# A float32 megakernel (conditioned mix, one-key attention, grouped convolution, 4-bit linear layer): the exponential of the mixing weights issued earlier, more products that nothing reads before the first z, and a new order of the calls on every engine

## The reference, cut to what matters

```
# stage 1
att   = softmax(MLP(cond))                       # [64, 8], a mixing weight for 8 kernels
m     = einsum('bk,koi,bih->boh', att, weight, x) + (att @ bias_k)
q,k,v = m @ Wq, m @ Wk, m @ Wv (+ biases)         # 32 heads for q, one for k and v
p     = softmax over e of q[s,d,h] * k[s,e] / sqrt(32)
o     = sum over e of p * v                       # copied to all heads: the reference sums q over heads
x     = x + o (each value on 32 neighbours)
# stage 2
u     = conv1d(x, 9 taps, 4 groups) + cond @ c_weight + bias
x     = x + u @ (scale * (int4 weights - zero)) + bias
```

## Time and profile before

| | us |
|---|---|
| median of 3 runs (lowest to highest) | 408.34 (408.29 to 411.07) |
| the execution that was profiled | 410.41 |
| its span, first to last instruction | 408.6 |
| PE busy / DVE busy / POOL busy / ACT busy | 390.6 / 352.2 / 294.1 / 217.6 |
| mean granted clock of TensorE, as a share of the full one | 0.987 |

### The profile page before, as it was taken

How to read it: one execution, slowest core, us unless ns; L and a number is a source line. 1 busy time by engine, 2 the same in 40 slices (tenths; PEclk the granted TensorE clock), 3 DMA queues, 4 the chain that set the end, 5 groups by cost and what they waited for, 6 DMA issues and landing times.

```text
span 408.6 us, 7642 instructions
## 1 busy us (share of the span) xinstructions
PE 390.6 (96%) x2747; PEld 306.1 (75%) x2747; DVE 352.2 (86%) x594; ACT 217.6 (53%) x472; POOL 294.1 (72%) x222
## 2 busy tenths in 40 slices
PE   5985987999999999999999999999999999999997
PEld 4875875878678778787867686878787786878686
DVE  1889998999999999999999899999999998963432
ACT  4535664765746483555656564747092826472600
POOL 6032988988829997589769987679948598519930
PEclk9999888999999999999999999999999999999999
DMA  8994994565176263729855434857146535525112
GB/s 317 408 408 178 346 335 148 171 265 187 45 269 226 93 208 106 262 90 319 288 166 209 127 110 136 310 170 275 55 143 226 168 147 158 184 82 205 56 53 104
DMA packets 24957, 79.20 MB, mean 194 GB/s; under 512 B 6088, under 2 KB 6728, under 8 KB 22984
## 3 DMA queue, kind: packets, MB, share of 16 engines
q1 hardware_dynamic: 24760, 78.32, 54.8%
q10 hardware_dynamic: 144, 0.13, 0.1%
HBM read 61.14 MB, written 17.30 MB: 192 GB/s over the span
## 4 chain that ended last, share of the span: by engine, by line
PE 44%; POOL 5%; issue 3%; DMA 2%; DVE 0%; SPq 0%; POOLq 0%; DVEq 0%
PE p_f L1913 32%; PE p_conv L1888 5%; PE p_conv L1897 4%; PE p_sm L1855 2%; POOL c_lo L594 2%; POOL xc L588 2%; DMA o_dram<-o_sb 1%; POOL xn L603 1%; DMA o_c<-o_dram 1%; POOL xn L610 1%; PE p_conv L1913 0%; PE p_sm L1875 0%; SPq L358 0%; DVE xn L1366 0%; DVE rden L1338 0%
## 5 line engine op out<-in xcount | busy, mean ns | idle before, releaser
L1913 PE MATMUL p_f<-w_ffn,u_hi 128*128 128x512 f32 (+1 forms) x512 | 195.6, 393 | 0.0
L1913 PE MATMUL p_f<-w_ffn,u_lo 128*128 128x512 f32 (+1 forms) x512 | 195.2, 390 | 0.0
L916 ACT ACTIVATE u_sb<-p_conv,u_bias,cols_sb 128x128 f32<-128x128 f32 x256 | 95.1, 481 | 83.3 <-PE p_conv L1897 81.6
L1913 PEld LDWEIGHTS p_f<-w_ffn,u_hi 128*128 128x128 f32 x512 | 96.1, 188 | 29.1 <-issue 9.0
L1913 PEld LDWEIGHTS p_f<-w_ffn,u_lo 128*128 128x128 f32 x512 | 96.1, 188 | 20.4 <-issue 0.8
L594 POOL TENSOR_TENSOR c_lo<-xc,c_hi 128x512 fp32r<-128x512 f32 (+1 forms) x68 | 76.1, 1139 | 23.0 <-ACT c_hi L906 23.0
L603 POOL TENSOR_TENSOR xn<-xn,bias_n 128x1024 f32<-128x1024 f32 x32 | 76.4, 2399 | 19.3 <-DMA xn<-xn_in_in 19.3
L588 POOL TENSOR_TENSOR xc<-xc,o_c 128x512 f32<-128x512 f32 (+1 forms) x68 | 69.6, 1050 | 26.6 <-DMA o_c<-o_dram 22.7
L1366 DVE TENSOR_TENSOR xn<-p_f,xn 128x512 f32<-128x512 f32 x64 | 43.2, 676 | 25.3 <-PE p_f L1913 18.4
L610 POOL TENSOR_TENSOR xn<-xn,o_sb 128x1024 f32<-128x1024 f32 x32 | 61.1, 1920 | 0.8
L895 ACT ACTIVATE prob<-prob 128x1024 f32<-128x1024 f32 (+1 forms) x32 | 34.0, 1063 | 37.4 <-DVE prob L1298 32.8
(11 more groups left out here) (124 smaller groups left out, 370.9 us busy)
## 6 DMA issues: line engine op xcount, KB each, us to landing
xn<-xn_in_in SPq DMA_DIRECT2D x16, 1024.0 KB, 5.7
out<-xn SPq DMA_DIRECT2D x31, 512.0 KB, 5.0
xc<-xc_in_in SPq DMA_DIRECT2D x15, 1040.0 KB, 7.1
xt<-xt_in_in SPq DMA_DIRECT2D x11, 1024.0 KB, 8.4
o_c<-o_dram SPq DMA_DIRECT2D x15, 256.0 KB
xn<-xt_in_in SPq DMA_DIRECT2D x3, 1024.0 KB, 16.6
xn<-wq_in SPq DMA_DIRECT2D x5, 512.0 KB, 8.4
xt<-xt_in_in SPq DMA_DIRECT2D x4, 512.0 KB, 10.9
```

Of the source, the lines that this page charges most:

```text
L916: ins = eng.activation(u_sb[:, g % 2, i * P:(i + 1) * P], p_conv[g][:, i * P:(i + 1) * P], ACT.Identity, bias=u_bias[:, g, bat:bat + 1], s ...
L1913: return mm(ffn_ps(k, part), u[:, (k // TU) % 2, r, t * P:(t + 1) * P], w_ffn[:, r, at:end], **flags)
```

## The change

No function is changed; only the lists of calls are. Three places stand out, the rest is a new order of calls on all engines (some 700 lines of the diff).

- ACT: `exp_att` is issued ahead of `copy_vk`, and DVE unpacks all nibbles directly behind the first sum of heads, for which SP loads `packed` as the third transfer and not the thirteenth.
- PE: 23 calls of `keep_busy(1)` in place of 14. They now also stand between the slices of `z_first`.
- All engines: calls in a new order, of which the first part stands here.

```diff
@@ SP @@
             load_wq(0)
+            load_packed()
             load_wq(1)
...
             load_wq(8)
-            load_packed()
             load_tile(0, 1)
             load_tile(1, 0)
-            load_c_first(0)
             load_conv_weights()
             load_tile(1, 1)
             load_x(2)
             load_x(3)
+            load_c_first(0)
             load_x(4)
             load_x(5)
+            load_bias()
             save_o(0, 0)
-            load_bias()
+            load_c_first(1)
             spread_first(0)
+            load_x(6)
+            load_n(0)
+            load_n(1)
             save_o(0, 1)
-            load_n(0)
-            load_x(6)
-            load_c_first(1)
             spread_first(1)
@@ POOL @@
             add_o(1, 0)
             add_o(1, 1)
+            x_o(0)
+            add_o(1, 2)
+            c_low(1, 0)
             x_bias(1)
-            c_low(1, 0)
-            add_o(1, 2)
             add_o(1, 3)
-            x_o(0)
-            x_o(1)
-            x_bias(2)
             c_low(1, 1)
             c_low(1, 2)
+            x_o(1)
             c_low(1, 3)
-            x_bias(3)
             add_o(2, 0)
             add_o(2, 1)
             add_o(2, 2)
+            c_low(2, 0)
+            x_bias(2)
@@ ACT @@
             keep_bias()
+            exp_att()
             copy_vk()
-            exp_att()
             slices()
...
             z_copy(0)
+            convert_weights(0, 0)
             exp(0, 0)
             exp_first()
+            exp(0, 1)
             z_copy(1)
-            exp(0, 1)
-            z_copy(2)
-            convert_weights(0, 0)
-            z_copy(3)
             exp(1, 0)
             bias_of_u()
+            z_copy(2)
+            exp(1, 1)
+            z_copy(3)
+            z_copy(4)
@@ DVE @@
             sum_heads(0)
+            low_nibbles()
+            high_nibbles()
             logits()
             normal()
             sum_heads(1)
             sum_heads(2)
             sum_heads(3)
-            mark_inexact()
...
             sum_heads(8)
-            low_nibbles()
+            mark_inexact()
             bias_of_qkv(0)
...
             sum_v_first()
-            softmax_top(1)
             divide(0, 0)
             sum_exp(0, 1)
+            softmax_top(1)
...
             sum_exp(1, 0)
-            high_nibbles()
             times_v(1, 0)
-            softmax_top(2)
             sum_v(1, 0)
             divide(1, 0)
             sum_exp(1, 1)
+            softmax_top(2)
...
             subtract(2, 1)
-            turn_u(0, 0)
             softmax_top(3)
             sum_exp(2, 0)
+            turn_u(0, 0)
@@ PE @@
             keep_busy(1)
             keep_busy(1)
             keep_busy(1)
+            keep_busy(1)
+            keep_busy(1)
+            keep_busy(1)
+            mlp(0)
             bias_rows()
-            mlp(0)
+            keep_busy(1)
             mlp(1)
+            keep_busy(1)
+            keep_busy(1)
             mlp(2)
             keep_busy(1)
             keep_busy(1)
             keep_busy(1)
             keep_busy(1)
+            keep_busy(1)
             turn_att()
+            keep_busy(1)
+            keep_busy(1)
+            keep_busy(1)
             z_first(0)
-            z_first(1)
             mixing(0)
             mixing(1)
             mixing(2)
             mixing_bias()
-            keep_busy(1)
-            keep_busy(1)
-            read_flag()
             mixing(3)
             keep_busy(1)
-            keep_busy(1)
-            keep_busy(1)
+            z_first(1)
             keep_busy(1)
             z_first(2)
+            keep_busy(1)
             z_first(3)
+            keep_busy(1)
             z_first(4)
+            keep_busy(1)
             z_first(5)
+            keep_busy(1)
             z_first(6)
-            keep_busy(1)
             z_first(7)
...
             project(1, 1)
+            context()
             mix(1)
             project(2, 0)
             project(2, 1)
-            context()
             project(3, 0)
             project(3, 1)
             mix(2)
             project(4, 0)
             project(4, 1)
-            conv(0, 0)
             project(5, 0)
             project(5, 1)
+            project(6, 0)
+            project(6, 1)
+            mix(3)
+            read_flag()
+            conv(0, 0)
             conv(0, 1)
             conv(0, 2)
             conv(0, 3)
-            project(6, 0)
             edges(0)
-            project(6, 1)
-            mix(3)
             project(7, 0)
             project(7, 1)
             project(8, 0)
+            project(8, 1)
             conv(1, 0)
             conv(1, 1)
             conv(1, 2)
             conv(1, 3)
             edges(1)
-            project(8, 1)
             linear(0, 0)
```

753 lines of the change are left out of this document (375 added, 378 removed).

## The result

The changed kernel takes 405.63 us in the median of 20 runs (403.28 to 412.64), the kernel before 408.78 of 20 runs beside it (406.76 to 411.07): a ratio of 0.9927, interval 0.9907 to 0.9947. The gain is 1.2 to 3.2 us where 7.1 were forecast (408.34 less 401.2), and the single runs of the changed kernel lie further apart than those of the one before. The profiled execution took 407.03 us with a span of 405.2.

What follows compares the result with a forecast made beforehand. Bound: the 72.3 us up to the first linear, plus a block where PE works without a gap. Gain 5.4 + 2.7 = 8.1 us gives 402.3 from the profile, 400.2 from the median, middle 401.2; range 398.5 to 406.3.

Steps and rivals of the forecast that it cites:

- rival D: Whole kernel: nothing is gained at the start and the new order only shuffles, within 1%, 408 us; chance 0.08.
- Part 3: PE from T0: project(7) at 55.9, first linear at 65.1, 7.1 us earlier, "in old times" (T0 left at 22.22).
- T0: Start of attention, the bias of q, k, v on DVE: 22.22 before, forecast at 19.5.
- Part 1: The start up to T0: the last head sum at 18.9 plus 0.62 us gives 19.5, gain 2.7 us.
- The head sums: DVE ahead of T0: packed delays Wq by 1.3 us, sums end 18.5 to 19.0 against 18.3, loss taken as 0.5.
- The clock at the start: PE with 23 keep_busy: high clock by about 10 to 14 us, so PE keeps up with the head sums.
- rival A: PE's start: the clock doesn't rise earlier, T0 at 22.7, total gain 4.9, 404.4 us; chance 0.17.
- High nibbles: DVE's unpacking, moved to the start: 0.67 to 1.50 us there, and 1.4 us leaves the chain behind T0.
- Part 2: DVE from T0 to 72 us: high nibbles leave, the 1.69 us wait goes, turn_u(0,0) moves; together 3.5 us ahead.
- PE keeps 5.4 of 7.1: Behind 72 us: PE keeps between 3.5 and 7.1 us of its lead, the middle taken as 5.4.
- Rival B: Behind the first linear: DVE bounds all, PE keeps 3.5 of 7.1, gain 6.2, 403.1 us; chance 0.19.
- C: DVE from 90 to 360 us: reordered calls wait at the queue's head, slower, for example 416 us; chance 0.04.

Runs made afterwards that it cites:

- second comparison: The unedited changed kernel run again against the kernel before, with the experiments: 407.28 us against 408.45, ratio 0.9946.
- a_oldpe: Changed kernel with PE's calls up to z_first(7) as in the kernel before (14 keep_busy, old places; read_flag at its new place): 407.27 us, ratio 0.9948.
- a_save: Changed kernel with load_n(1) issued behind save_o(0,1) on SP: 403.79 us, ratio 0.9883.
- a_fill: Changed kernel with products that nothing reads on PE, 12 ahead of mix(1) and 7 ahead of mix(2): 407.54 us, ratio 0.9942.
- best: Changed kernel with packed behind load_wq(8), both unpackings behind divide(0,0), convert_weights(0,0) behind z_copy(1), load_n(1) behind save_o(0,1): 405.28 us, ratio 0.9928.
- after_look: The changed kernel, unedited, a third profile: 406.03 us, span 404.2.
- after_again: The changed kernel, unedited, run and profiled again: 407.28 us, ratio to the kernel before 0.9946.
- a_x7: Changed kernel with load_x(7) issued ahead of save_o(0,1) on SP: 407.85 us, ratio 0.9968.
- best_fill18: The kernel of best with products that nothing reads on PE, 12 ahead of mix(1) and 18 ahead of mix(2): 403.97 us, ratio 0.9853.

## Why the prediction was wrong

The direction held, and so did the place: what is won is won ahead of the first linear. The size did not: 401.2 forecast, 405.6 measured, inside the range (the second comparison's 407.3 is outside it), and by under 1%, which I had given to rival D. The step that failed is Part 3, project(7) "at 55.9", through the tile that it waits for and the clock that it then runs at; T0, Part 1, fell short beside it.

- **The head sums (part 1, "taken as 0.5").** This term was mis-sized: they end at 20.05, 1.75 us later, and the experiment without the early packed has them at 17.66. I delayed only the last piece; pieces before it came too late for their sums as well, so DVE waited twice, 0.80 and 1.25 us. T0 is 20.81, 20.94 and 20.46 in three profiles, for 19.5: 1.0 to 1.4 us. Why that is more than the 1.3 us of the transfer put ahead of them, no run takes apart.
- **The clock at the start** rose by about 10 us, as forecast, and mixing(3) ended at 13.4 to 14.5. But it was not what T0 waited for: with the old products, where the weight loads of a column sum still take 0.40 us for four at 18.0, T0 is 21.14 (a_oldpe), 0.3 us later than with the new ones. And rival A is part of the truth in another form: the clock may rise too early, be lost at turn_att, and T0 then comes at 24 (a_save, a_fill). I had costed the products both ways ("4.7 us of PE at the low clock and half at the high one") but not asked whether, at half their time, they still cover the wait for turn_att.
- **High nibbles.** 0.69 us, by the lower bound (0.67). In all four profiles in which it starts 1 us behind POOL's `prob` it takes 1.50 and ends 0.5 to 0.6 us behind that one; behind divide(0,0), with no POOL instruction beside it, 0.69 (best). At the start it isn't alone, but there it came first, and it is POOL that took longer. POOL in the first profile of the changed kernel:

```profile
6.98 0.75 POOL L572 CAST rest_hi<-zp 128x128 fp32r<-128x128 f32 x1
7.82 0.75 POOL L574 TENSOR_TENSOR rest_lo<-zp,rest_hi 128x128 fp32r<-128x128 f32 x1
```

  The same two take 0.29 and 0.40 us in the kernel before, where DVE unpacks nothing beside them. The Trainium skill, SBUF — State Buffer, section "SBUF: two separate sides", has an exclusive lock by which the later of the two blocks; the rows agree, in both directions.
- **Part 3, project(7) "at 55.9" in old times**, 53.2 with the forecast T0. This is the step that failed. I had seen save_o(0,1) behind load_n(1) and priced it for conv(1) alone (63.6); that load_x(7) stands behind the same spread was missed. Measured 57.38: 1.3 of the difference from T0, 2.9 from the tile. Then project(7) at the low clock: 4.51 for 2.86, 1.6 us. Together 5.8, all of the difference between 62.4 and 68.17. In the two other profiles of the same kernel the tile costs less: T0, tile and what follows project(7) come to 1.0, 1.8 and 1.6 us in after_look, 1.4, 0.3 and 0.4 in after_again. Without the tile the step was right: in a_x7 project(7) waits for DVE alone and starts 33.8 us behind T0, where the forecast had 33.7. Putting load_n(1) behind save_o(0,1) takes the wait for the tile away (a_save, best, best_fill18); what that is worth at the end isn't shown, as a_save has 0.9883 and best, with the same repair among others, 0.9928.
- **The clock in the middle.** I took it as given (2.9 "or 4.5 where the clock is low"). It differed by execution: the first linear was 64.60, 66.72 or 68.17 with T0 at 20.5 to 20.9. In two profiles of before it varied by 0.1.
- **Part 2.** The 1.69 us wait of turn_u(1,0) for u_copy(1,0) is gone as forecast. But a new one of 2.45 us stands a few rows earlier: it is turn_u(0,3) that waits, for u_copy(0,3), which the new order on ACT has behind z_copy(7), and so behind project(7). So a late project(7) holds up DVE too. DVE in the first profile of the changed kernel:

```profile
63.64 0.46 DVE L1352 STREAM_TRANSPOSE p_conv<-u_sb 128x256 f32<-128x256 f32 x1 [2.45 <-ACT u_sb L916]
...
69.74 0.78 DVE L1352 STREAM_TRANSPOSE p_conv<-u_sb 128x256 f32<-128x256 f32 x2
```

  POOL's wait for xn ahead of c_low(1,1) is gone as forecast; it waits 2.00 us for c_high there now.
- **"PE keeps 5.4 of 7.1"**, a loss of 1.7 us (the middle of 3.5 and 7.1 is 5.3), came out about right in size: the end is 337.3 us behind the first linear on average where it was 335.9, a loss of 1.4. That is luck, as the reason was another: I had DVE lag by more the further PE runs ahead, and the loss doesn't grow with the lead. What it consists of is open; the waits of PE behind 72 us explain 0.5 us of it in the first profile. Rival B, a loss of 3.6, fell (DVE's busy time from 60 to 360 is 285.80, before 286.12), and C, slower, with it; D's size came, but not its mechanism, as T0 and the first linear are both earlier. With a first linear at 62.4 and 337 us behind it the span would have been 399.4; with the mean of the three measured, 66.5, it is 403.5, and 405.3 with the 1.8 us around the span. On top of that come the runs with the late start, 9 of 32, which no term of the sum holds.
- **Profile against median.** Two profiled executions of before took 410.4 and 409.8, its median is 408.8: the middle that I took between them was right in kind. The changed kernel's three took 407.0, 403.4 and 406.0.
- Attention's last o is at 356.63, for a forecast of 351 to 354, 2.8 earlier than before.

What stays open: why the clock rises before 5.2 us in some executions and near 10 in others; where the spread of the kernel before comes from, whose runs have a mean granted clock of 0.983 to 0.992 and take 406.2 to 412.3 us; and what of the 0.75% between best and best_fill18 is the full clock and what the small number of runs on another chip. That falls follow idle time of PE is borne out by best_fill18, where the waits are filled and all six runs are without a fall; which idle time brings one is not (a_fill fell after two waits of 0.5 us, best held through 1.74). That the late start costs some 3 us is seen in T0 of a_save and a_fill (24.0 and 24.4) and in the medians of the 9 and the 23 runs (409.0 and 405.5).

## What to carry to other kernels

- When a call moves on an in-order DMA queue, list everything behind it up to the next wait of the compute engine, not only the transfer that it was moved for: here one load ahead of one save delayed a tile that PE waited for, and ACT and POOL behind it.
- Products that keep the clock up are issued by number, and take half as long once it is up: count those ahead of a wait at the high clock (0.28 us for a pair of records; at the low one it is 0.50, ten records in 2.50 us in after_look), or shorten the chain that TensorE waits for.
- Before pricing what follows, check whether one engine is full from some point on; if so, the moment it starts is what matters most (here all but 1.4 us of the lead was kept). Look at more than one profile of a kernel in which waits of TensorE of a few microseconds lie ahead of that point, and at the mean granted clock of the runs that weren't profiled.

## What the runs showed of the hardware

- The clock's course is not a property of the kernel alone: identical instructions had the first low stretch end between 33 and 34 us in one execution and near 36.7 in another, and of these two the one with the longer low stretch ended earlier (401.6 against 405.2): PE came to the next wait later and stood for 0.28 us in place of 1.72. It isn't a rule; after_look has the longer stretch too, falls at project(7) all the same and ends at 404.2. The Trainium skill, TensorE: Matmul & The Clock Gate, Part 1, says that the point of rising differs between runs of one kernel; here the rise came before 5.2 us in some profiles (two records in 0.49 us at 5.12 in a_save) and near 10 in others, which agrees.
- Equal waits don't always bring a fall: 1.72 us ahead of mix(2) did in the first profile of the changed kernel, 1.74 us at the same place in best did not (1.00 from 36 us on), and in a_oldpe the clock stood through 2.75 us at mix(1) and fell after 3.22 at mix(2). And short ones can be enough: a_fill fell at 56 us after two of 0.44 and 0.51. Idle time makes the fall possible; which execution has it is not in the kernel's text.
- At the start of the program the windows print a clock of 1.00 in both cases; only the lengths tell them apart (ten records in 1.38 us, or in 2.20 to 2.50).
- DVE's unpacking and a POOL instruction beside it don't share: the one that starts later takes longer, 1.50 us for 0.69 on DVE, 0.75 for 0.29 on POOL.
- The exponential started at 8.60, 0.10 us after its table load of 1.28 us ended at 8.50. The Trainium skill, ScalarE: Activation LUTs, section "What ACT_TABLE_LOAD costs", puts a further 1.38 us to each switch; on this row nothing of that is to be seen behind the load.
